# Softmax sums of a latent attention stage: the two halves of the keys added on VectorE, two batches summed in one pair of products, three probability tiles for four

## The reference, cut to what matters

```python
xn, ln_lat = layer_norm(ctx_1024, g1, b1), layer_norm(x, g2, b2)
q, kv = ln_lat @ Wq, concatenate([xn, ln_lat], axis=1) @ Wkv
...
weight = einsum('bhld,bhnd->bhln', q * scale, k * scale)
weight = where(full_mask, weight, neg)
weight = softmax(weight, axis=-1)          # over 128 keys
out = einsum('bhln,bhnd->bhld', weight, v)
x = layernorm(x + out @ Wout)
```

## Time and profile before

| | us |
|---|---|
| median of three runs | 1608.52 (1604.91 to 1608.94) |
| the profiled execution | 1607.23, span 1605.4 |
| its stretch with steps 2 to 63 | 972 to 1532 |
| its tail (last shares, last feed-forward) | 1532 to 1605 |

### The profile page before, as it was taken

One profiled execution on the slowest core, in us unless ns is written; L12 is line 12 of the kernel. 1 busy time (PEld: TensorE's weight loads), 2 busy tenths in 40 slices (PEclk: granted clock), 3 DMA queues, 4 the chain that ended last, 5 costly groups with the idle time before them and its releaser, 6 DMA issues. The chain is left out here.

```text
span 1605.4 us, 32269 instructions
## 1 busy us (share of the span) xinstructions
PE 1424.4 (89%) x12643; PEld 868.5 (54%) x12658; DVE 1134.2 (71%) x2363; ACT 963.8 (60%) x1498; POOL 303.9 (19%) x278
## 2 busy tenths in 40 slices
PE   7999999998999788878887868999999999999962
PEld 4666666665664333334333345566666666666541
DVE  4666778885336799889988943445667767766788
ACT  2332367675555988789878944345556665555433
POOL 3434335352001100111010031111112211110101
PEclk9999999997999999999999979999999999999995
DMA  4000000001000000000000002222222222222210
GB/s 178 2 2 2 2 19 12 15 6 54 1 1 1 1 2 1 1 1 1 1 1 4 1 14 53 62 68 65 61 60 60 66 67 68 65 57 57 69 47 17
DMA packets 41013, 50.78 MB, mean 32 GB/s; under 512 B 9248, under 2 KB 23200, under 8 KB 40480
## 3 DMA queue, kind: packets, MB, share of 16 engines
q1 hardware_dynamic: 40576, 48.06, 11.7%
q10 hardware_dynamic: 288, 0.67, 0.1%
HBM read 13.04 MB, written 2.10 MB: 9 GB/s over the span
## 5 line engine op out<-in xcount | busy, mean ns | idle before, releaser
L1836 DVE TENSOR_TENSOR l_px<-psum,l_share 128x1024 f32<-128x1024 f32 x64 | 78.4, 1224 | 154.6 <-PE psum L1552 104.6
L1694 ACT ACTIVATE l_prob<-psum,l_bias 128x1024 f32<-128x1024 f32 x64 | 71.3, 1115 | 172.5 <-PE psum L1529 172.5
L1541 PE MATMUL psum<-l_XT,l_A 128*128 128x256 f32 x512 | 126.3, 391 | 3.3 <-ACT l_XT L1709 3.1
L1524 PE MATMUL psum<-l_th,l_XT 128*128 128x512 f32 x256 | 125.6, 613 | 1.4 <-DVE stream L1843 0.7
L1588 PE MATMUL psum<-l_px,l_N 128*128 128x256 f32 x512 | 124.2, 386 | 1.8 <-ACT l_r L1735 1.8
L1552 PE MATMUL psum<-l_prob,l_X 128*128 128x512 f32 x256 | 122.8, 603 | 0.0
L1817 DVE TENSOR_REDUCE l_top<-psum 128x8 bf16<-128x1024 f32 x64 | 78.2, 1221 | 43.6 <-PE psum L1603 43.5
L895 PE MATMUL psum<-f_projX,f_kT 64*128 64x512 f32 x256 | 77.1, 679 | 34.1 <-DVE f_frac L1266 18.6
L1588 PEld LDWEIGHTS psum<-l_px,l_N 128*128 128x128 f32 x512 | 94.0, 191 | 19.1 <-issue 4.7
L1541 PEld LDWEIGHTS psum<-l_XT,l_A 128*128 128x128 f32 x512 | 93.6, 193 | 15.0 <-ACT l_XT L1709 3.6
L1266 DVE TENSOR_TENSOR f_frac<-psum,f_whole 128x1024 f32<-128x1024 f32 x80 | 98.0, 1225 | 2.7
(11 more groups left out here) (309 smaller groups left out, 3198.9 us busy)
## 6 DMA issues: line engine op xcount, KB each, us to landing
l_share<-l_recip SPq DMA_DIRECT2D x512, 64.0 KB, 2.0
early_weights<-in_weights SPq DMA_DIRECT2D x1, 2405.0 KB, 11.2
c_cs<-in_ctx SPq DMA_DIRECT2D x16, 128.0 KB, 2.1
f_qf<-in_l_mats SPq DMA_DIRECT2D x1, 2048.0 KB, 8.0
out<-l_normed SPq DMA_DIRECT2D x16, 128.0 KB, 2.0
l_craw<-in_ctx SPq DMA_DIRECT2D x15, 128.0 KB, 2.3
late_weights<-in_weights SPq DMA_DIRECT2D x1, 1089.0 KB, 11.2
relbias<-in_relbias ACTq DMA_DIRECT2D x1, 512.0 KB, 5.2
```

Of the source, the lines that this page charges most:

```text
L1524: nc.tensor.matmul(ps[:, SC + n, :], XT[:, q % 3, k, :, :], th[:, q % 2, k, 8 * n:8 * n + 8, :], start=True, stop=False)
L1541: last = nc.tensor.matmul(ps[:, at + j // 2, (j % 2) * 256:(j % 2 + 1) * 256], A[:, QB * k + j, :], XT[:, q % 3, :, 1, :], start=True, sto ...
L1836: nc.vector.tensor_tensor(px[:, q % 2, :, k, :], ps[:, GA:GA + 2, :].rearrange("p a (h s) -> p (a h) s", s=S), share[:, (b // 2) % 2, b % ...
```

## The change

A new DVE instruction, `fold(b)`, adds for each batch the probabilities of partitions 0 to 63 and 64 to 127 (64 x 1024 elements) into one half of a tile `half`: partitions 0 to 63 for an even batch, 64 to 127 for an odd one. It waits for `exponent(b)`, stands in DVE's queue just ahead of `divide(b-2)`, and DVE waits for its own result before it goes on. `sums(p)` then needs two products instead of four: `half` holds both batches, and the weight `sides` (64 columns) has ones in rows 0 to 63 for columns 0 to 31 and in rows 64 to 127 for columns 32 to 63. Its wait is now on `folded`, not on `exped`. The sums land in other rows: column group 0 in rows 0 to 63 (batch 2p, then batch 2p+1), column group 1 in rows 64 to 127 (the same). `spread` still goes through n = 0 to 3 in order, but a block is now batch n % 2 and column group n // 2. The ring of `l_prob` has three tiles, and `exponent(b)` waits for the gather and the fold of batch b-3. Three small memsets make `sides` once.

```diff
--- before.py
+++ after.py
@@ -1413,7 +1413,7 @@
...
-        "d_ps d_read var3 root3 normed stored0 stored1 steps asteps").split()}
+        "d_ps d_read var3 root3 normed stored0 stored1 steps asteps folded sides").split()}
@@ -1440,7 +1440,8 @@
     X = sb("X", [P, 2, QB, P])
     th, th16 = sb("th", [P, 2, QB, H, S]), sb("th16", [P, 2, QB, H, S], BF16)
     top = sb("top", [P, 4, PAIRS], BF16)
-    prob = sb("prob", [P, 4, 2, 512])
+    prob = sb("prob", [P, 3, 2, 512])
+    half, sides = sb("half", [P, 2, 512]), sb("sides", [P, 64])
     recip, turned, small = sb("recip", [P, 2, 512]), sb("turned", [P, 512]), sb("small", [P, 16])
     share = sb("share", [P, 2, 2, 2, 512])
     px = sb("px", [P, 2, H, QB, S])
@@ -1482,8 +1483,8 @@
                     sp.wait_ge(s["px_sb"], 2 * p - 2)
                 for n in range(4):
                     for m in range(4):
-                        sp.dma_start(share[32 * m:32 * m + 32, p % 2, n // 2, n % 2, :], recip[32 * n:32 * n + 32, p % 2, :]
-                                     ).then_inc(s[f"share{n // 2}{p % 2}"], 16)
+                        sp.dma_start(share[32 * m:32 * m + 32, p % 2, n % 2, n // 2, :], recip[32 * n:32 * n + 32, p % 2, :]
+                                     ).then_inc(s[f"share{n % 2}{p % 2}"], 16)
 
             def store(q):
                 sp.wait_ge(s["normed"], q + 1)
@@ -1549,17 +1550,17 @@
                 if b >= 1:
                     pe.wait_ge(s["px_sb"], b)
                 for n in range(2):
-                    last = nc.tensor.matmul(ps[:, GA + n, :], X[:, q % 2, k, :], prob[:, b % 4, n, :], start=True, stop=True)
+                    last = nc.tensor.matmul(ps[:, GA + n, :], X[:, q % 2, k, :], prob[:, b % 3, n, :], start=True, stop=True)
                 last.then_inc(s["px_ps"], 1)
 
             def sums(p):
-                pe.wait_ge(s["exped"], 2 * p + 2)
+                pe.wait_ge(s["folded"], 2 * p + 2)
+                if p == 0:
+                    pe.wait_ge(s["sides"], 2)
                 if p >= 1:
                     pe.wait_ge(s["sums_read"], p)
-                for b in range(2):
-                    for n in range(2):
-                        at = 32 * (2 * b + n)
-                        last = nc.tensor.matmul(ps[at:at + 32, SU, :], ones32[:, 0:32], prob[:, (2 * p + b) % 4, n, :], start=True, stop=True)
+                for n in range(2):
+                    last = nc.tensor.matmul(ps[64 * n:64 * n + 64, SU, :], sides[:, :], half[:, n, :], start=True, stop=True)
                 last.then_inc(s["sums"], 1)
 
             def columns_in(q):
@@ -1688,10 +1689,10 @@
                 act.wait_ge(s["scores"], b + 1)
                 if b == 0:
                     act.wait_ge(s["masked"], 1)
-                if b >= 4:
-                    act.wait_ge(s["px_ps"], b - 3)
-                    act.wait_ge(s["sums"], b // 2 - 1)
-                nc.scalar.activation(prob[:, b % 4, :, :], ps[:, SC:SC + 2, :], ACT.Exp, bias=bias[:, b:b + 1]).then_inc(s["exped"], 1)
+                if b >= 3:
+                    act.wait_ge(s["px_ps"], b - 2)
+                    act.wait_ge(s["folded"], b - 2)
+                nc.scalar.activation(prob[:, b % 3, :, :], ps[:, SC:SC + 2, :], ACT.Exp, bias=bias[:, b:b + 1]).then_inc(s["exped"], 1)
 
             def keep_heads(q, k):
                 act.wait_ge(s["th_ps"], QB * q + k + 1)
@@ -1951,6 +1952,21 @@
                 nc.vector.tensor_tensor(rstd2[:, LATE], rstd2[:, LATE], rstd[:, LATE], ALU.mult).then_inc(s["prep"], 1)
                 dve.wait_ge(s["prep"], 5)
 
+            def fold(b):
+                dve.wait_ge(s["exped"], b + 1)
+                if b >= 2 and b % 2 == 0:
+                    dve.wait_ge(s["sums"], b // 2)
+                at = b % 2 * S
+                nc.vector.tensor_tensor(half[at:at + S, :, :], prob[0:S, b % 3, :, :], prob[S:P, b % 3, :, :], ALU.add
+                                        ).then_inc(s["folded"], 1)
+                dve.wait_ge(s["folded"], b + 1)
+
+            def sides_made():
+                nc.vector.memset(sides[:, :], 0.0).then_inc(s["sides"], 1)
+                dve.wait_ge(s["sides"], 1)
+                nc.vector.memset(sides[0:S, 0:32], 1.0)
+                nc.vector.memset(sides[S:P, 32:64], 1.0).then_inc(s["sides"], 1)
+
             def weights_measured():
                 nc.vector.memset(ones32[:, :], 1.0)
                 nc.vector.memset(eps[:, :], EPS_NORM)
@@ -1976,6 +1992,7 @@
             for i in range(FIRST, LAST):
                 if i == -7:
                     weights_measured()
+                    sides_made()
                 if i == -3:
                     weights_quantised()
                 if 0 <= i < B:
@@ -1994,6 +2011,8 @@
                     down_moments(job(i, 23))
                 if job(i, -9) is not None:
                     prepare(job(i, -9))
+                if 0 <= i < B:
+                    fold(i)
                 if 0 <= i - 2 < B:
                     divide(i - 2)
                 if i % 2 == 1 and 0 <= i < B:
```

## The result

| | before | after |
|---|---|---|
| median, four runs each | 1606.72 us (1603.36 to 1608.94) | 1705.99 us (1700.15 to 1713.01) |
| the profiled execution, and its span | 1607.23, 1605.4 | 1709.77, 1708.0 |
| mean granted clock of PE | 0.964 | 0.948 |

The changed kernel takes 1.0621 of the time of before (95% interval 1.0594 to 1.0649), 99 us more by the medians and 102.5 by the profiled executions. The forecast was +84, 1691, in 1658 to 1722. Sign and range hold; the size is 15 short.

A forecast was written before the change was run, and what follows sets the result against it. PE was taken to set the pace, with the DMA path of the shares nearly as long. Shares 56, fold 12, sums -3 and clock 19 made +84 us on 1607.2, that is 1691, range 1658 to 1722.

The forecast's parts named there:

- Shares: Even batch's divide on DVE waits for DMA issue 12, not 8, 2.53 us later; PE's shift waits behind it: +56 us.
- the two ends: The 11 pairs at the kernel's start and end lose 1.1 to 2.5 us each to late share DMAs: 20 us.
- Clock: Longer PE waits drop its clock from 2.4 to 1.2 GHz: 11 falls at 1.7 us lost each, +19 us.
- Fold and sums: Fold on DVE costs 12 us, mainly by PE's sums waiting; the two new products on PE gain 3.
- the clock holds: Rival: PE's granted clock does not fall in the longer waits, giving 1672 us; chance 0.24.
- a fall in every round: PE's clock falls in every round with a long wait: 17 x 1.7 = 29 us in place of 19.
- DVE has room: In steps 2 to 63 DVE is busy 361 of 560 us, 440 with folds, so it does not become the bound.
- Sums: Two 64-column products on PE run together in 0.95 us, against 1.00 for four: 3 us gained.
- the rival of 1716: Rival: the two new products of sums on PE don't run together, +25 us over 32 pairs: 1716; chance 0.06.
- Four steady steps: Time of four steps in the steady part goes from 37.1 to about 41.2 us, 42.5 with clock falls.
- The rival with hidden shares: Rival: issue order doesn't set when the share DMAs land, so only the fold remains: 1616 us; chance 0.05.
- the faster one: Rival: two products of sums on PE cost half of four, 16 us gained, late shares and fold hidden: 1591; chance 0.02.

The follow-up runs named there:

- e10: Kernel before with its share DMA blocks issued in order 0, 2, 1, 3, plus 32 useless products in PE's wait; no fold: 1669.46 us, 1.0407.
- e3: Changed kernel with 32 small products, read by nobody, put on PE ahead of the shift in its long wait for row maxima: 1687.16 us, 1.0489.
- e1: Changed kernel with share DMA blocks issued in order 0, 2, 1, 3, so the even batch's two come first: 1619.74 us, 1.0072.
- e2: Kernel before with share DMA blocks issued in order 0, 2, 1, 3, making the even batch's second block late; no fold, no new sums: 1690.38 us, 1.0510.
- e5: e1 with the fold moved ahead of `prepare` in DVE's queue, so that PE's sums need not wait for it: 1619.91 us, 1.0074.
- e4: Kernel before with two 64-column products of sums for the four of 32, reading only the odd batch's probabilities: 1608.58 us, 0.9996.
- e7: Kernel before with the even batch's second block of four share DMAs issued by ACT, the other twelve by SP: 1600.71 us, 0.9952.

## Why the prediction was right, and where it was short

- **Shares**, forecast 56, measured 65 by e10. The mechanism is as told: issue 12 for issue 8, 2.53 us, and the divide at 9.73 us, where 9.7 to 9.8 was forecast. In the 32 steps from 24 to 56 the working holds nearly to the letter. Each kind of step grew in e10 by 2.30 us (kind 0; forecast 2.4), 0.94 (kind 2; 0.75) and 0.0 and -0.1 (kinds 1 and 3), together 25.0 us; the terms of the sum for these steps are 25.2. What was short are the two ends, each by 3 to 4 us: in e10 the time from the maxima of step 0 to those of step 24 grew by 23.6 us (the terms of the sum for it are some 20), from step 56 to 63 by 11.5 (8.2), and the tail behind the last maxima by 6.3 (2.5; in the changed kernel 6.8).
- **Long issues** were in no term. The step that failed is "Its divide waits for issue 12, not issue 8: 6.89 - 4.36 = 2.53 us later": read from one burst, it takes every burst for a regular one. Over the pairs of the changed kernel the mean gap is 10.16, where 9.75 was taken. 0.41 x 32 is 13 us at most; in e10 it was 9.84, 3 us.
- **Clock**, forecast 19, measured 16 to 21 (19 by the medians of e3). The size is right, its working only in part. Of the 12 waits in kind 1 that it counted seven had a fall, of the four at the ends three; but four of the seven, and all three at the ends, were waits of 2.98 us or longer, not of 2.4, and four more falls came before scores, which the working did not count: 14 falls for 11. The share of four in six was also read short: the second phase of the kernel before has seven waits of 2.1 us (that at 556.80 is left out, its four products take 1.63 us) and seven of 2.17 us, and its clock fell near seven of these 14. Nor do the falls count in full: at 1.7 us for each 3.4 us they make 27 us, and e3 gave back 16 to 21. The rival, the clock holds, is out: the mean in the steps is 0.96. So is a fall in every round, 29 us.
- **Fold and sums**, forecast 12 - 3 = 9, measured 11 by e1. The fold took 1227 ns, where 1.23 was forecast. In the changed kernel the cost lies where it was forecast: steps of kind 3 grew by 1.09 us (forecast 1.1; 0.79 in e3 with the clock held), and without a fold, in e2 and e10, by 0.10 and -0.12. As a reason the wait of the sums on PE is only one part. With the shares early they do wait 0.8 us for the fold in kind 3 (e1), but e5 takes that wait away and gains nothing. Under it lies a second path of nearly the same length: inversion 0.69 later, shares later, divide released by the DMA. The prediction had written of that DMA path that it has 0.1 us to spare, and did not apply it to the fold. That "DVE has room" held for its sum and not for the 8 us between maxima and inversion.
- **Sums**, forecast -3, measured 0: 1.07 to 1.09 us for 0.95, and the four products before take 1.07 too; the 1.00 of the working is their piece in the chain. They run together, as told, so the rival of 1716 is out too; the measured median lies near it for other reasons.
- **Four steady steps** were forecast to take 42.5 us with the clock falling. The 32 steps from 24 to 56 grew by 47.0 us, 5.9 in four, from 37.3 to 43.2. In the changed kernel kind 0 grew by 2.36, kind 1 by 0.88, kind 2 by 1.56, kind 3 by 1.09. With the clock held, in e3 and e10, kind 1 is at 0.0: its 0.88 is the slow clock behind the wait.

The range was written as reaching up to the high bound, which is 1726 in the working, and given as ending at 1722; the result lies below either.

Together: 65 (e10) + 19 (e3) + 11 (e1) = 95 of 99. The 4 left are inside the intervals of these runs, and less than what the mean gaps of e10 and of the changed kernel differ by (0.32 x 32 = 10), so they need no further cause; they are not shown to be this one. The rival with hidden shares falls with e1 and e2, and so does the faster one.

## What to carry to other kernels

When a change renames the rows of an intermediate tile, look at the order in which a queue moves them: here the layout of the sums, an aside of the change, cost 82 us, and the reordered loop of e1 takes nearly all of it back. Two paths that end within 0.1 us of each other must both be followed for every instruction that is added ahead of either; taking one wait away (e5) then shows the other and gains nothing. Halving the instructions of a product that already spreads over idle columns of the array halves nothing, so it can't pay for an instruction elsewhere.

## What the runs showed of the hardware

- Four f32 products with 32 columns of weight and 512 moving ones take 1.00 to 1.07 us (before), two with 64 columns 1.07 to 1.09 (e4 and the changed kernel), two of full width 1.72.
- In the steps of the changed kernel 14 of PE's 20 waits of 1.97 to 3.99 us went with 3.4 or 6.8 us at 1.2 GHz: 6 of the 11 up to 2.46 us, 8 of the 9 from 2.98 us on. Four waits of 1.61 to 1.86 us did not. 32 products without a use, put into one wait of each four steps (e3), kept the clock at 1.00 and made the kernel 19 us faster.
- An issue on SP that normally takes 0.59 us takes 1.1 to 1.8 in 11 of the 32 bursts of sixteen of the changed kernel, at recurring places of the program, and a divide that needs the issue before it can come 1.5 us later (3.64 us after issue 12 for 2.10). With twelve of the sixteen on SP and four on ACT (e7) no gap of pairs 7 to 28 showed it.
- Adding 64 x 1024 f32 elements whose two inputs lie in different halves of the partitions takes 1227 ns, as much as the divide on 128 partitions does (1225).
